# Attention and routed experts on one core: value products of a third query group in two parts, a pair of maxima and a transpose moved, and the last tiles taken two at a time

## The chip, the cores and the metric

The kernel runs on one core of a Trainium2 chip. The metric is device time in microseconds (us) of one execution; the kernel before takes 240.64 us, the median of 3 runs.

## What is computed

`x` is 2048 rows of 128 features. After a layer norm (`xn`), two branches are added to `x`: an attention over all 2048 rows with one head of 128 features, and a mixture of 8 experts of which each row takes two.

```python
xn = layernorm(x)
q, k, v = split(xn @ w_qkv.T)              # 2048 x 128 each
probs = softmax(q @ k.T / sqrt(8))
attn = swapaxes(probs @ v).reshape(...) @ w_proj.T + b_proj
t = xn @ W_in + b_in
gate: softmax(t @ W_gate + b_gate), the best two, normalised
moe = sum over the two experts of gate * (relu(t @ W1[e] + b1[e]) @ W2[e] + b2[e])
out = x + attn + (moe @ W_out + b_out)
```

## The kernel before

TensorE (PE) holds the order of the work, and the other engines have lists of their own that meet it at semaphores.

**Attention.** The 2048 queries are in six groups g: four of 256 (0 to 3) and two of 512 (4 and 5). A group is worked off in steps k (`STEPS`: 8 for a group of 256, 16 for one of 512), numbered i over the whole kernel, so group 2 is steps 16 to 23 and group 3 is steps 24 to 31. A step has 512 columns of scores: two blocks of 128 keys for a group of 256, one for a group of 512. In it PE does

- `scores(i)`: three products of a block of keys with the queries (lines 845 to 847). Numbers are kept as a high and a low part in fp32r: high times high, high times low, low times high.
- sometimes a *pair*, `pair(g + 1, m)` (line 906): raw scores of the next group, 128 queries by 1024 keys in two banks of PSUM. VectorE (DVE) takes the maximum of them (`pair_max`, line 618), and the next pair may only be written when that has been read (`max_read`), since all pairs of a later group use the same two banks. `PAIR_STEP[g]` lists in which steps the pairs stand; of two in one step the second stands behind the value products.
- `values(i - 2)`: the probabilities of two steps ago times the normed rows. In groups 0 to 3 this is one fp32 product for each block (line 970) of the probabilities `pf` that ScalarE (ACT) wrote (line 465). In groups 4 and 5 ACT writes the exponential twice, rounded to fp32r (`ph`, line 464) and whole (`pf`), DVE takes the difference `pl` (`low`, line 628), and PE does three fp32r products (lines 979, 980, 983).
- behind the last steps' work, the group before is finished: ACT copies its sums (`copy_u`, line 477), PE multiplies by the value weights (`out_rows`, line 997), DVE divides (`scale_out`, lines 634 and 637), PE multiplies by `w_proj` (`project`, line 1011), DVE adds (`add_out`, line 645).

**Routing.** GpSimd (POOL) sends the rows of `t` to slots in memory, sorted by expert, with 32 scatters (line 365), among them the additions of the bias (line 338) and the first four copies of expert weights (`stage`, line 355). When all scatters have landed, SyncE's queue (SP) loads the first tiles of slots (`load_xg`, line 266).

**Experts.** After group 3, 39 tiles of 128 slots go through the experts: a transpose of the tile (`xg_transpose`, line 1075, into one bank, so that each waits for ACT's copy of the one before; the first also waits until all maxima of group 4 are read), `layer1` (line 1087), `layer2` (line 1101). SP stores each result. Between group 3's last value products and the experts stand

```python
            values(BASE_B - 2)
            xg_transpose(0)
            xg_transpose(1)
            values(BASE_B - 1)
            layer1(0)
```

**The last part.** Groups 4 and 5 run on PE, and meanwhile POOL fetches the two results of each row back: for each of 16 tiles j two gathers (line 392) and the product of the one before with its first gate (`weigh`, line 387). DVE adds the second (`combine`, line 784). After the last `combine`, PE transposes the last four tiles (line 1134), DVE copies them (`cT`, line 815), and the last four row tiles are finished one by one (`last_scale`, lines 821 and 822; `last_add`, line 828; PE lines 1175, 1183, 1186). SP stores them in two transfers (line 289).

Of the kernel before, what the change touches and what calls it, by code (L numbers as in the profile page):

```python
# [7 lines left out]
ALU = mybir.AluOpType  # L8
# [4 lines left out]
def attention_moe_kernel(nc, x, w_qkv, w_proj, b_proj, w_in, b_in, w_gate, b_gate,  # L13
# [4 lines left out]
    P = 128  # L18
    S, D = x.shape[1], x.shape[2]
    NT = S // P  # L20
# [19 lines left out]
    PRE = 4  # L40
    WHOLE = 4

    PAIR_STEP = [[2, 4, 5, 6]] + 2 * [[1, 2, 4, 5]] + [[1, 2, 3, 4, 5, 6, 7, 7], [1, 3, 5, 6, 8, 9, 11, 12], []]
    NG = len(GROUPS)
# [10 lines left out]
    LAST = FIRST[NG]  # L55
    PLAIN = FIRST[WHOLE]

# [8 lines left out]
    def group_of(i):  # L66
        return max(g for g in range(NG) if FIRST[g] <= i)

    def pairs_at(g, k):
        return [m for m, at in enumerate(PAIR_STEP[g]) if at == k]  # L70

# [4 lines left out]

    BLOCK_AT = {14: 0, 21: 1, 28: 2}

    ctx = ExitStack()
    with ctx:  # L80
# [136 lines left out]

        def row_bank(c):  # L220
            return (MA, 0, 1, 2)[c]

        def sum_bank(c):
            return (MB, MX + 1, MA, 0)[c]

# [6 lines left out]
        def _(sp):  # L232
# [53 lines left out]
            for c in (2, 4):  # L286
                sp.wait_ge(Z["last_added"], c)
                a = NT - TB + c - 2
                sp.dma_start(ov[:, a:a + 2, :], x_sb[:, a:a + 2, :]).then_inc(Z["stored"], 16)
# [3 lines left out]
        def _(pool):  # L293
# [96 lines left out]
            for j in range(NT):  # L390
                for c in range(TOPK):
                    pool.indirect_dma_start(out=z[:, j, c, :], out_offset=None, in_=slots_out,  # L392
                                            in_offset=bass.IndirectOffsetOnAxis(ap=slots[:, c, j:j + 1], axis=0)
                                            ).then_inc(s_z[j], 16)
                if j >= 1:
                    weigh(j - 1)
            weigh(NT - 1)

        @block.scalar
        def _(act):  # L400
# [59 lines left out]
            def step(i):  # L460

                act.wait_ge(Z["st_done"], i + 1)
                if i >= PLAIN:
                    act.activation(ph[:, i % 3, :], ps[:, st_bank(i), :], ACT.Exp).then_inc(Z["ph_done"], 1)  # L464
                act.activation(pf[:, i % 3, :], ps[:, st_bank(i), :], ACT.Exp).then_inc(Z["pf_done"], 1)  # L465

            def copy_u(g):
                n = SIZE[g]
                act.wait_ge(Z["pv_done"], g + 1)
                if g >= 1:  # L470
                    act.wait_ge(Z["out_done"], FIRST_ROUND[g])
                parts = TILES[g] if g == NG - 1 else 1
                to = ut[:, 0:n].rearrange("e (p j) -> e j p", j=NT)
                of = ps[:, UB, 0:n].rearrange("e (j p) -> e j p", j=NT)
                for c in range(parts):
                    w = n // NT // parts
                    act.activation(to[:, :, w * c:w * (c + 1)], of[:, :, w * c:w * (c + 1)], ACT.Copy).then_inc(Z["ut_copied"], 1)
# [67 lines left out]
        def _(dve):  # L545
# [185 lines left out]
            for g in range(PRE):  # L731
                for k in range(STEPS[g]):
# [7 lines left out]
                    if k == PAIR_STEP[g][-1]:  # L740
                        row_max(g + 1)
                    if FIRST[g] + k >= PLAIN:
                        low(FIRST[g] + k)
# [36 lines left out]
            def combine(j):  # L780

                dve.wait_ge(s_z[j], 32)
                dve.wait_ge(Z["z_weighed"], j + 1)
                dve.scalar_tensor_tensor(out=z[:, j, 0, :], in0=z[:, j, 1, :], scalar=gate2[:, j:j + 1],
                                         in1=z[:, j, 0, :], op0=ALU.mult, op1=ALU.add).then_inc(Z["c_ready"], 1)
# [31 lines left out]

            def last_scale(c):
                n = FIRST_ROUND[NG - 1]
                dve.wait_ge(Z["out_done"], n + 1 + c)  # L820
                link("rinv", dve.reciprocal(rinv[:, c // 2, c % 2:c % 2 + 1], ps[:, row_bank(c), D:D + 1]))
                dve.tensor_scalar(o_sb[:, c // 2, c % 2, :], ps[:, row_bank(c), 0:D], rinv[:, c // 2, c % 2:c % 2 + 1], None,
                                  ALU.mult).then_inc(Z["o_ready"], 1)

            def last_add(c):
                at = x_sb[:, NT - TB + c, :]
                dve.wait_ge(Z["proj_done"], FIRST_ROUND[NG - 1] + c + 1)
                dve.tensor_tensor(at, ps[:, sum_bank(c), 0:D], at, ALU.add).then_inc(Z["last_added"], 1)

# [3 lines left out]
            last_scale(1)  # L833
            last_scale(2)
            last_add(0)
            last_scale(3)
            last_add(1)
            last_add(2)
            last_add(3)

        @block.tensor
        def _(pe):
# [116 lines left out]
            def values(i):  # L959
# [5 lines left out]
                elif first and g > 0:  # L965
                    pe.wait_ge(Z["ut_copied"], g)
                if g < WHOLE:
                    pe.wait_ge(Z["pf_done"], i + 1)
                    for h, c in enumerate(keys(i)):
                        last = pe.matmul(dst, xn[:, c, :], pf[:, i % 3, cols(g, h)], start=(first and h == 0),  # L970
                                         stop=(final and h == CH[g] - 1))
                    if final:
                        last.then_inc(Z["pv_done"], 1)
                    return
                pe.wait_ge(Z["ph_done"], i - PLAIN + 1)
                if g == WHOLE:
                    pe.wait_ge(Z["xnn_lo_ready"], keys(i)[-1] // TB + 1)
                for h, c in enumerate(keys(i)):
                    pe.matmul(dst, xn_hi[:, c, :], ph[:, i % 3, cols(g, h)], start=(first and h == 0), stop=False)
                    pe.matmul(dst, xn_lo[:, c, :], ph[:, i % 3, cols(g, h)], start=False, stop=False)  # L980
                pe.wait_ge(Z["lo_done"], i - PLAIN + 1)
                for h, c in enumerate(keys(i)):
# [189 lines left out]
            pe.wait_ge(Z["x_added"], NG - 1)  # L1172
            for c in range(TB):
                pe.wait_ge(Z["ut_copied"], NG + c)
                pe.matmul(ps[:, row_bank(c), 0:D + 2], ut[:, P * c:P * (c + 1)], wvT[:, :], start=True, stop=True
                          ).then_inc(Z["out_done"], 1)
# [7 lines left out]
            for c in range(TB):  # L1184
# [30 lines left out]
```

## Time and profile before

| | |
|---|---|
| median of 3 runs | 240.64 us (240.54 to 240.68) |
| the profiled execution, its own time | 240.99 us |
| its span, first to last instruction | 239.2 us |
| PE busy | 224.5 us, 94% |
| VectorE, ScalarE, GpSimd busy | 58%, 46%, 59% |
| granted clock of TensorE | full speed (its upper level, 2.4 GHz) in every slice |

Busy time of PE is the sum of its matmul records, whose ends are modelled, so a stretch that is full of work shows nearly 100%; what a stretch is worth is read from the starts of its rows. A record gives the duration of one matmul from its first column to its last result, while the next starts in its shadow: the distance between two starts is what a matmul costs. An fp32 matmul is two records. DMAs that SP and POOL issue have rows of their own; a gather or a scatter row is the time in which POOL makes its descriptors.

### The profile page before, as it was taken

How to read it: one execution, taken by the hardware profiler on the slowest of the kernel's cores; microseconds unless marked ns; L12 is line 12 of the kernel's file. 1: busy time of each engine (PE TensorE's matmuls, PEld its weight loads, DVE VectorE, ACT ScalarE, POOL GpSimd, SP SyncE). 2: the span in 40 equal slices, each digit the busy share in tenths (PEclk: the TensorE clock that was granted, in tenths of full speed). 3: DMA queues.
4: the chain of work that ended last, by engine and by line, in shares of the span. 5: the costliest groups of instructions: out<-in, count | busy, mean ns of one | idle time of the engine just before them, and what ended most of it. 6: DMA issues, size and time to landing. Idle time of an engine off the chain costs nothing.

```text
span 239.2 us, 4415 instructions
## 1 busy us (share of the span) xinstructions
PE 224.5 (94%) x1526; PEld 203.0 (85%) x1526; DVE 138.1 (58%) x332; ACT 110.1 (46%) x260; POOL 140.5 (59%) x163
## 2 busy tenths in 40 slices
PE   8798988999999997999999999999999989899974
PEld 8587876999999995899999999999977768688853
DVE  4988795552551754434445444445498885656644
ACT  2481432424325331544544444554466657667640
POOL 3249005888888850136666555666048888888830
PEclk9999999999999999999999999999999999999999
DMA  6799910111111103012222222222102111313121
GB/s 181 283 319 342 323 42 25 50 39 47 34 44 47 44 33 88 11 36 66 70 73 73 67 79 67 68 67 67 36 25 56 33 44 48 76 34 80 40 66 47
DMA packets 23046, 19.53 MB, mean 82 GB/s; under 512 B 3280, under 2 KB 19696, under 8 KB 22768
## 3 DMA queue, kind: packets, MB, share of 16 engines
q1 hardware_dynamic: 20000, 14.71, 20.3%
q0 software_dynamic: 2048, 4.20, 6.6%
q10 hardware_dynamic: 976, 0.33, 0.5%
q8 instruction: 13, 0.21, 0.3%
q14 instruction: 9, 0.07, 0.1%
HBM read 10.97 MB, written 8.26 MB: 80 GB/s over the span
## 4 chain that ended last, share of the span: by engine, by line
PE 59%; POOL 19%; DVE 9%; issue 6%; DMA 3%; ACT 2%; ACTq 1%; POOLq 0%; DVEq 0%
PE ps L1101 15%; PE ps L1087 15%; POOL wtab L392 14%; PE ps L970 9%; POOL wtab L387 5%; PE ps L906 4%; DVE part_max L618 4%; PE ps L845 3%; PE ps L847 3%; PE ps L846 3%; DMA w_raw<-in_L_attn_w_proj_dram 2%; PE ps L1075 2%; PE ps L872 1%; PE ps L997 1%; DMA slots_out<-y_sb 1%
## 5 line engine op out<-in xcount | busy, mean ns | idle before, releaser
L355 POOL COPY wst<-wtab 128x1156 f32 x39 | 44.9, 1151 | 39.7 <-DVE y_sb L766 39.7
L465 ACT ACTIVATE pf<-ps 128x512 f32<-128x512 f32 x64 | 38.1, 595 | 36.1 <-PE ps L847 32.5
L618 DVE TENSOR_REDUCE part_max<-ps 128x1 f32<-128x1024 f32 x32 | 38.8, 1222 | 13.2 <-PE ps L906 11.4
L365 POOL DMA_INDIRECT slots_in<-hl,slots x32 | 31.5, 985 | 20.1 <-DVE slots L698 13.2
L392 POOL DMA_INDIRECT wtab<-slots_out,slots x32 | 33.3, 1040 | 15.9 <-DMA slots_out<-y_sb 8.4
L1101 PE MATMUL ps<-wst,mid 128*128 128x128 f32 x312 | 41.3, 275 | 0.7 <-DVE x_sb L645 0.7
L1087 PE MATMUL ps<-xgT,wst 128*128 128x128 f32 x312 | 41.3, 275 | 0.0
L758 DVE TENSOR_SCALAR mid<-ps,wst 128x128 f32<-128x128 f32 x78 | 23.7, 346 | 29.7 <-PE ps L1087 29.7
L1101 PEld LDWEIGHTS ps<-wst,mid 128*128 128x128 f32 x312 | 38.0, 192 | 0.9 <-ACT mid L509 0.8
L1087 PEld LDWEIGHTS ps<-xgT,wst 128*128 128x128 f32 x312 | 38.0, 192 | 0.1
L845 PE MATMUL ps<-q_hi,xnT_hi 128*128 128x256 f32 (+1 forms) x96 | 35.6, 371 | 0.5 <-ACT q_hi L451 0.5
L970 PE MATMUL ps<-pf,xn 128*128 128x256 f32 x128 | 32.9, 379 | 0.0
L847 PE MATMUL ps<-q_lo,xnT_hi 128*128 128x256 f32 (+1 forms) x96 | 30.6, 318 | 0.0
L628 DVE TENSOR_TENSOR pl<-pf,ph 128x512 fp32r<-128x512 f32 x32 | 22.8, 713 | 13.3 <-ACT pf L465 11.9
L846 PE MATMUL ps<-q_hi,xnT_lo 128*128 128x256 f32 (+1 forms) x96 | 30.5, 317 | 0.0
L464 ACT ACTIVATE ph<-ps 128x512 fp32r<-128x512 f32 x32 | 19.2, 599 | 19.6 <-PE ps L847 18.1
L509 ACT ACTIVATE mid<-ps,wst 128x128 f32<-128x128 f32 x78 | 24.3, 363 | 7.5 <-PE ps L1087 7.5
L502 ACT ACTIVATE xgT<-ps 128x128 f32<-128x128 f32 x39 | 10.8, 278 | 34.7 <-PE ps L1075 34.7
L970 PEld LDWEIGHTS ps<-pf,xn 128*128 128x128 f32 x128 | 23.5, 189 | 3.6
L906 PE MATMUL ps<-xnT_hi,q_hi 128*128 128x512 f32 x64 | 21.0, 412 | 2.9 <-DVE part_max L618 2.4
L845 PEld LDWEIGHTS ps<-q_hi,xnT_hi 128*128 128x128 f32 x96 | 18.2, 189 | 2.3 <-ACT q_hi L451 0.7
L846 PEld LDWEIGHTS ps<-q_hi,xnT_lo 128*128 128x128 f32 x96 | 18.2, 189 | 1.6
(156 smaller groups left out, 309.5 us busy)
## 6 DMA issues: line engine op xcount, KB each, us to landing
wtab<-in_L_ffn_W_dram SPq DMA_DIRECT2D x16, 256.0 KB, 5.9
xg<-slots_in SPq DMA_DIRECT2D x39, 64.0 KB, 1.9
slots_out<-y_sb SPq DMA_DIRECT2D x39, 64.0 KB, 1.5
slots_in<-wst SPq DMA_DIRECT2D x2, 1024.0 KB, 4.9
x_sb<-in_L_attn_x_dram SPq DMA_DIRECT2D x4, 256.0 KB, 5.1
out_dram<-x_sb SPq DMA_DIRECT2D x3, 256.0 KB
wtab<-in_L_ffn_b_dram SPq DMA_DIRECT2D x1, 512.0 KB, 7.4
slots_in<-hl,slots POOLq DMA_INDIRECT x32
```

What stands on the lines that cost most here:

```text
L355: pool.tensor_copy(wst[:, t % 4, :], wtab[:, bass.ds(experts[t], 1), :].rearrange("p a n -> p (a n)")).then_inc(Z["staged"], 1)
L365: pool.indirect_dma_start(out=slots_in, out_offset=bass.IndirectOffsetOnAxis(ap=slots[:, c, j:j + 1], axis=0), in_=hl[:, j, 0:D], in_offse ...
L392: pool.indirect_dma_start(out=z[:, j, c, :], out_offset=None, in_=slots_out, in_offset=bass.IndirectOffsetOnAxis(ap=slots[:, c, j:j + 1], ...
L465: act.activation(pf[:, i % 3, :], ps[:, st_bank(i), :], ACT.Exp).then_inc(Z["pf_done"], 1)
L618: dve.tensor_reduce(part_max[:, g % 2, m // 2, m % 2:m % 2 + 1], ps[:, b:b + 2, :], AX.XY, ALU.max).then_inc(Z["max_read"], 1)
L845: pe.matmul(dst, lh, rh, start=start, stop=False)
L846: pe.matmul(dst, ll, rh, start=False, stop=False)
L847: return pe.matmul(dst, lh, rl, start=False, stop=stop)
L906: last = pe.matmul(ps[:, pair_bank(g, m) + b, :], q_hi[:, g % 2, P * t:P * (t + 1)], xnT_hi[:, at:at + BK], start=True, stop=True)
L970: last = pe.matmul(dst, xn[:, c, :], pf[:, i % 3, cols(g, h)], start=(first and h == 0), stop=(final and h == CH[g] - 1))
L1087: last = pe.matmul(ps[:, 2 * (t % 2) + h, SL * (c % 2):SL * (c % 2 + 1)], wst[:, t % 4, P * c:P * (c + 1)], xgT[:, t % 2, :], start=True, ...
L1101: last = pe.matmul(ps[:, y_bank(t), 0:D], mid[:, t % 2, c, :], wst[:, t % 4, DM + D * c:DM + D * (c + 1)], start=(c == 0), stop=(c == HC - 1))
```

## The change

Four edits are made together.

1. `WHOLE` becomes a set, groups 0, 1 and 3. Group 2 now splits its probabilities as groups 4 and 5 do; `splits(i)` counts the steps that do so.
2. In group 3, the list of pairs has its double step at step 6 where it was at step 7, and `values(BASE_B - 1)` stands between the first two transposes of slot tiles.
3. POOL weighs tiles 0 to 13; for tiles 14 and 15 DVE does it in `combine`.
4. The last four row tiles are scaled, projected and added two at a time, in one bank for two; the product with `wo_sb` stands beside the one with `wpT` that adds to it.

```diff
-    WHOLE = 4
+    WHOLE = (0, 1, 3)
-    PAIR_STEP = [[2, 4, 5, 6]] + 2 * [[1, 2, 4, 5]] + [[1, 2, 3, 4, 5, 6, 7, 7], [1, 3, 5, 6, 8, 9, 11, 12], []]
+    PAIR_STEP = [[2, 4, 5, 6]] + 2 * [[1, 2, 4, 5]] + [[1, 2, 3, 4, 5, 6, 6, 7], [1, 3, 5, 6, 8, 9, 11, 12], []]
+    def splits(i):
+        return sum(group_of(s) not in WHOLE for s in range(i + 1))
+    WEIGHED = 14
...
-                if j >= 1:
+                if 1 <= j <= WEIGHED:
                     weigh(j - 1)
-            weigh(NT - 1)
...
-                if i >= PLAIN:
+                if group_of(i) not in WHOLE:
                     act.activation(ph[:, i % 3, :], ps[:, st_bank(i), :], ACT.Exp).then_inc(Z["ph_done"], 1)
...
-                parts = TILES[g] if g == NG - 1 else 1
+                parts = ROUNDS[g] if g == NG - 1 else 1
...
-                    if FIRST[g] + k >= PLAIN:
+                    if g not in WHOLE:
                         low(FIRST[g] + k)
...
-                dve.wait_ge(Z["z_weighed"], j + 1)
+                if j < WEIGHED:
+                    dve.wait_ge(Z["z_weighed"], j + 1)
+                else:
+                    link("rinv", dve.tensor_scalar(z[:, j, 0, :], z[:, j, 0, :], gate1[:, j:j + 1], None, ALU.mult))
...
-            def last_scale(c):
+            def last_scale(r):
+                n = FIRST_ROUND[NG - 1] + r
+                rows = ps[:, row_bank(r), 0:2 * (D + 2)].rearrange("q (k d) -> q k d", d=D + 2)
+                dve.wait_ge(Z["out_done"], n + 1)
+                link("rinv", dve.reciprocal(rinv[:, n % 2, :], rows[:, :, D]))
+                dve.tensor_tensor(o_sb[:, n % 2, :, :], rows[:, :, 0:D], rinv[:, n % 2, :].unsqueeze(2).to_broadcast([P, 2, D]),
                                   ALU.mult).then_inc(Z["o_ready"], 1)
...
             last_scale(0)
             last_scale(1)
-            last_scale(2)
             last_add(0)
-            last_scale(3)
             last_add(1)
-            last_add(2)
-            last_add(3)
...
-                pe.wait_ge(Z["ph_done"], i - PLAIN + 1)
-                if g == WHOLE:
+                pe.wait_ge(Z["ph_done"], splits(i))
+                if g == min(set(range(NG)) - set(WHOLE)):
                     pe.wait_ge(Z["xnn_lo_ready"], keys(i)[-1] // TB + 1)
...
             xg_transpose(0)
+            values(BASE_B - 1)
             xg_transpose(1)
-            values(BASE_B - 1)
...
-            for c in range(TB):
-
-                if c >= 2:
-                    pe.wait_ge(Z["o_ready"], n + c - 1)
-                pe.matmul(ps[:, sum_bank(c), 0:D], cT[:, P * c:P * (c + 1)], wo_sb[:, :], start=True, stop=False)
-            for c in range(TB):
-                pe.wait_ge(Z["o_ready"], n + 1 + c)
-                pe.matmul(ps[:, sum_bank(c), 0:D], o_sb[:, c // 2, c % 2, :], wpT[:, :], start=False, stop=True
-                          ).then_inc(Z["proj_done"], 1)
+            for r in range(ROUNDS[NG - 1]):
+
+                pe.wait_ge(Z["o_ready"], n + r + 1)
+                for k in range(2):
+                    at = P * (2 * r + k)
+                    pe.matmul(ps[:, sum_bank(r), P * k:P * (k + 1)], cT[:, at:at + P], wo_sb[:, :], start=True, stop=False)
+                    last = pe.matmul(ps[:, sum_bank(r), P * k:P * (k + 1)], o_sb[:, (n + r) % 2, k, :], wpT[:, :], start=False, stop=True)
+                last.then_inc(Z["proj_done"], 1)
```

TensorE's list at the end of group 3, before: from the pair of step 7 (line 906) to the first `layer1` (line 1087). Line 970 is a value product, line 1075 a transpose of slots.

```order
L906 MATMUL ps<-xnT_hi,q_hi 128x512 x2
L970 MATMUL ps<-pf,xn 128x256 x2
L906 MATMUL ps<-xnT_hi,q_hi 128x512 x2
L970 MATMUL ps<-pf,xn 128x256 x2
L1075 MATMUL ps<-ident,xg 128x128 x2
L970 MATMUL ps<-pf,xn 128x256 x2
L1087 MATMUL ps<-xgT,wst 128x128 x4
```

The same place now, from the second pair of step 6; lines 850 to 852 are the scores of step 31, line 911 a pair, 975 value products, 1080 a transpose, 1092 `layer1`.

```order
L911 MATMUL ps<-xnT_hi,q_hi 128x512 x2
L850 MATMUL ps<-q_hi,xnT_hi 128x256
L851 MATMUL ps<-q_hi,xnT_lo 128x256
L852 MATMUL ps<-q_lo,xnT_hi 128x256
L850 MATMUL ps<-q_hi,xnT_hi 128x256
L851 MATMUL ps<-q_hi,xnT_lo 128x256
L852 MATMUL ps<-q_lo,xnT_hi 128x256
L911 MATMUL ps<-xnT_hi,q_hi 128x512 x2
L975 MATMUL ps<-pf,xn 128x256 x4
L1080 MATMUL ps<-ident,xg 128x128
L975 MATMUL ps<-pf,xn 128x256 x2
L1080 MATMUL ps<-ident,xg 128x128
```

Behind the last pair stood one step's value products; two steps' stand there now, and the last step's are between the transposes.

VectorE's list in steps 1 to 4 of group 2, now. Line 622 is a maximum of a pair, 632 the new `low`, 638 and 641 the division (`scale_out`), 649 `add_out`; before, the same list stood there without the rows of `pl`.

```order
L622 TENSOR_REDUCE part_max<-ps 128x1
L632 TENSOR_TENSOR pl<-pf,ph 128x512
L622 TENSOR_REDUCE part_max<-ps 128x1
L632 TENSOR_TENSOR pl<-pf,ph 128x512
L638 RECIPROCAL rinv<-ps 128x2
L641 TENSOR_TENSOR o_sb<-ps,rinv 128x256
L632 TENSOR_TENSOR pl<-pf,ph 128x512
L649 TENSOR_TENSOR x_sb<-ps,x_sb 128x256
L622 TENSOR_REDUCE part_max<-ps 128x1
```

So the division of group 1 stands behind the difference of step 2, and the addition behind that of step 3.

## Rows read from the trace of the kernel before

**Rows 1.** The page: span, then busy us and share of each engine
```profile
span 239.2 us, 4415 instructions
PE 224.5 (94%) x1526; PEld 203.0 (85%) x1526; DVE 138.1 (58%) x332; ACT 110.1 (46%) x260; POOL 140.5 (59%) x163
```

**Rows 2.** The chain that ended last: start us, us, what
```profile
173.44 1.52 DMA slots_out<-y_sb
...
175.92 0.99 POOL wtab L392
...
228.99 1.84 issue
```

**Rows 3.** Timeline, PE, group 2, steps 1 to 3: start us, us, line
```profile
61.13 1.03 PE L970 MATMUL ps<-pf,xn 128*128 128x256 f32 x4
61.81 0.47 PE L845 MATMUL ps<-q_hi,xnT_hi 128*128 128x256 f32 x1
62.12 0.28 PE L846 MATMUL ps<-q_hi,xnT_lo 128*128 128x256 f32 x1
...
62.71 0.64 PE L906 MATMUL ps<-xnT_hi,q_hi 128*128 128x512 f32 x2
63.18 1.02 PE L970 MATMUL ps<-pf,xn 128*128 128x256 f32 x4
...
66.07 0.61 PE L1011 MATMUL ps<-wpT,o_sb 128*128 128x128 f32 x4
```

**Rows 4.** Timeline, DVE, the same steps
```profile
63.38 1.23 DVE L618 TENSOR_REDUCE part_max<-ps 128x1 f32<-128x1024 f32 x1 [0.82 <-PE ps L906]
...
64.90 0.42 DVE L637 TENSOR_TENSOR o_sb<-ps,rinv 128x256 f32<-128x256 f32 x1
```

**Rows 5.** Lines 628, 387 and 392, all their instructions: ns min/median/max
```profile
L628 DVE TENSOR_TENSOR pl<-pf,ph x32: 676/692/930, 173.4 to 229.1; 128x512 fp32r<-128x512 f32 x32
...
L387 POOL TENSOR_SCALAR wtab<-wtab,gate x16: 602/760/1082, 181.2 to 230.9; 128x128 f32<-128x128 f32 x16
...
L392 POOL DMA_INDIRECT wtab<-slots_out,slots x32: 944/1001/1462, 175.9 to 227.2; - x32
```

**Rows 6.** Timeline, PE, end of group 3
```profile
88.11 0.64 PE L906 MATMUL ps<-xnT_hi,q_hi 128*128 128x512 f32 x2
...
92.11 0.73 PE L906 MATMUL ps<-xnT_hi,q_hi 128*128 128x512 f32 x2 [0.45 <-DVE part_max L618]
92.68 1.02 PE L970 MATMUL ps<-pf,xn 128*128 128x256 f32 x4
94.25 0.30 PE L1075 MATMUL ps<-ident,xg 128*128 128x128 f32 x1 [0.55 <-DVE part_max L618]
95.01 0.30 PE L1075 MATMUL ps<-ident,xg 128*128 128x128 f32 x1 [0.46 <-ACT xgT L502]
95.15 1.03 PE L970 MATMUL ps<-pf,xn 128*128 128x256 f32 x4
96.01 1.05 PE L1087 MATMUL ps<-xgT,wst 128*128 128x128 f32 x8
```

**Rows 7.** Timeline, SP, first eight slot loads; page, DMA issues, last number us to landing
```profile
88.85 3.66 SPq L266 DMA_DIRECT2D xg<-slots_in  x8
...
xg<-slots_in SPq DMA_DIRECT2D x39, 64.0 KB, 1.9
```

**Rows 8.** Timeline, all engines, the tail
```profile
230.89 0.60 POOL L387 TENSOR_SCALAR wtab<-wtab,gate 128x128 f32<-128x128 f32 x1 [1.89 <-DMA wtab<-slots_out,slots]
231.59 0.35 DVE L784 SCALAR_TENSOR_TENSOR wtab<-wtab,gate 128x128 f32<-128x128 f32 x1 [1.50 <-POOL wtab L387]
...
232.69 0.69 DVE L815 COPY cT<-ps 128x512 f32<-128x512 f32 x1 [0.75 <-PE ps L1134]
...
235.92 0.49 PE L1186 MATMUL ps<-wpT,o_sb 128*128 128x128 f32 x2 [0.40 <-DVE o_sb L822]
...
236.45 0.29 DVE L828 TENSOR_TENSOR x_sb<-ps,x_sb 128x128 f32<-128x128 f32 x1 [0.19 <-PE ps L1186]
```

More of the change, by code:

```diff
@@ L55, in attention_moe_kernel @@
     LAST = FIRST[NG]
-    PLAIN = FIRST[WHOLE]
     BY_DVE = [2, 2, 3, 3]
@@ L216, in hl_banks, with row_bank, sum_bank @@
             return ps[:, b:b + 2, 0:2 * HW].rearrange("p b (j n) -> p b j n", n=HW)
[L220 to L224, printed above, removed]
+        def row_bank(r):
+            return (MA, 0)[r]
+        def sum_bank(r):
+            return (MB, MX + 1)[r]
         def y_bank(t):
@@ L285, in _ @@
                 sp.dma_start(ov[:, a:b, :], x_sb[:, a:b, :]).then_inc(Z["stored"], 16)
-            for c in (2, 4):
-                sp.wait_ge(Z["last_added"], c)
-                a = NT - TB + c - 2
+            for r in range(ROUNDS[NG - 1]):
+                sp.wait_ge(Z["last_added"], r + 1)
+                a = NT - TB + 2 * r
                 sp.dma_start(ov[:, a:a + 2, :], x_sb[:, a:a + 2, :]).then_inc(Z["stored"], 16)
@@ L815, in _, with last_add @@
             dve.tensor_copy(cT[:, :], ps[:, MX, :]).then_inc(Z["cT_copied"], 1)
-            def last_scale(c):
[L819 to L822, printed above, removed]
-                                  ALU.mult).then_inc(Z["o_ready"], 1)
[L825 to L828, printed above, removed]
+            def last_scale(r):
[4 more added lines that the diff above has]
+                dve.tensor_tensor(o_sb[:, n % 2, :, :], rows[:, :, 0:D], rinv[:, n % 2, :].unsqueeze(2).to_broadcast([P, 2, D]),
+                                  ALU.mult).then_inc(Z["o_ready"], 1)
+            def last_add(r):
+                at = x_sb[:, NT - TB + 2 * r:NT - TB + 2 * r + 2, :]
+                dve.wait_ge(Z["proj_done"], FIRST_ROUND[NG - 1] + r + 1)
+                dve.tensor_tensor(at, ps[:, sum_bank(r), 0:2 * D].rearrange("p (j e) -> p j e", e=D), at, ALU.add
+                                  ).then_inc(Z["last_added"], 1)
             dve.wait_ge(Z["proj_done"], FIRST_ROUND[NG - 1])
@@ L966, in values @@
                     pe.wait_ge(Z["ut_copied"], g)
-                if g < WHOLE:
+                if g in WHOLE:
                     pe.wait_ge(Z["pf_done"], i + 1)
@@ L980, in values @@
                     pe.matmul(dst, xn_lo[:, c, :], ph[:, i % 3, cols(g, h)], start=False, stop=False)
-                pe.wait_ge(Z["lo_done"], i - PLAIN + 1)
+                pe.wait_ge(Z["lo_done"], splits(i))
                 for h, c in enumerate(keys(i)):
@@ L1172, in _ @@
             pe.wait_ge(Z["x_added"], NG - 1)
-            for c in range(TB):
-                pe.wait_ge(Z["ut_copied"], NG + c)
-                pe.matmul(ps[:, row_bank(c), 0:D + 2], ut[:, P * c:P * (c + 1)], wvT[:, :], start=True, stop=True
-                          ).then_inc(Z["out_done"], 1)
+            for r in range(ROUNDS[NG - 1]):
+                pe.wait_ge(Z["ut_copied"], NG + r)
+                for k in range(2):
+                    at = P * (2 * r + k)
+                    last = pe.matmul(ps[:, row_bank(r), (D + 2) * k:(D + 2) * (k + 1)], ut[:, at:at + P], wvT[:, :], start=True, stop=True)
+                last.then_inc(Z["out_done"], 1)
             pe.wait_ge(Z["cT_copied"], NR)
             pe.wait_ge(Z["moe_added"], NR - 1)
-            for c in range(TB):
-                if c >= 2:
-                    pe.wait_ge(Z["o_ready"], n + c - 1)
-                pe.matmul(ps[:, sum_bank(c), 0:D], cT[:, P * c:P * (c + 1)], wo_sb[:, :], start=True, stop=False)
-            for c in range(TB):
-                pe.wait_ge(Z["o_ready"], n + 1 + c)
-                pe.matmul(ps[:, sum_bank(c), 0:D], o_sb[:, c // 2, c % 2, :], wpT[:, :], start=False, stop=True
-                          ).then_inc(Z["proj_done"], 1)
+            for r in range(ROUNDS[NG - 1]):
+                pe.wait_ge(Z["o_ready"], n + r + 1)
+                for k in range(2):
+                    at = P * (2 * r + k)
+                    pe.matmul(ps[:, sum_bank(r), P * k:P * (k + 1)], cT[:, at:at + P], wo_sb[:, :], start=True, stop=False)
+                    last = pe.matmul(ps[:, sum_bank(r), P * k:P * (k + 1)], o_sb[:, (n + r) % 2, k, :], wpT[:, :], start=False, stop=True)
+                last.then_inc(Z["proj_done"], 1)
 _INS = ['L0_attn_x', 'L0_attn_w_qkv', 'L0_attn_w_proj', 'L0_attn_b_proj', 'L0_ffn_W_in', 'L0_ffn_b_in',
```

## The prediction

> **What bounds the kernel now.** I read the page first: PE is busy 94% of a span of 239.2 us [rows 1]. A share over the whole says too little, so next the chain of waits, in order of time. It has three parts. Up to 173 us it is PE almost throughout: groups 0 to 3, then the 39 expert tiles. At 173.44 the last result goes to memory, and from 175.92 to 228.99 the chain is POOL's 32 gathers with 15 products between them [rows 2]; the steps of groups 4 and 5 run beside them and end a little earlier. Then comes the tail, from the landing of the last gather to the last addition [rows 8]. So an edit counts if it shortens PE's list before 173 us (all that follows is released by the last expert tile and moves with it) or the tail. For both I read the timeline engine by engine. The profiled execution took 240.99 us, 1.79 more than its span and 0.35 more than the median of 240.64; I take differences from its rows and subtract them from the median.
>
> **Group 2 in parts.** Before, a step's values are two fp32 products, 4 records. From the start at 61.13 to the scores at 61.81 are 0.68 us, and the first score product holds on 0.31 us (to 62.12) where the next five take (62.71 - 62.12) / 5 = 0.118: together 0.68 + 0.19 = 0.87 us [rows 3]. After, they are 6 fp32r products of 256 columns, the form of the scores: 6 x 0.118 = 0.71. That saves 0.16 a step, 8 x 0.16 = 1.28 us.
>
> What it adds lies on other engines. ACT: 8 more exponentials, of 0.6 us, which it has room for (busy 46% [rows 1]); the pair of step 1 needs the next queries' high part from behind one of them, and has some 0.2 us to spare by my count. DVE: 8 times `low`, median 0.69 [rows 5], in order between the pairs' maxima. Three places are close:
>
> - Step 2: the maximum starts at 63.38 [rows 4]. The `low` of step 1 stands ahead of it, behind a maximum that began one step of 2.05 us earlier and ended at 61.33 + 1.23 = 62.56, and so ends near 63.3: no delay.
> - Step 3: `project` started at 66.07 [rows 3]; two steps of shorter values would bring it to 65.75. It needs the division, which now stands behind the `low` of step 2. Before, the product of the division was over at 64.90 + 0.42 = 65.32 [rows 4]; a `low` in line costs some 0.55 to 0.62 (the next operation starts before its end), so 65.87 to 65.94. PE waits 0.15 to 0.2.
> - The next pair in the following step can start 0.67 (from pair to maximum, 62.71 to 63.38) + 1.23 + 0.06 (a hop) = 1.96 us after the one before [rows 3, 4]. The step was 2.05 long and becomes 1.89: 0.07 of waiting, in step 5 of group 2 and step 2 of group 3.
>
> The `low` of a step is done over a step before `values` asks for it. Together 1.28 - 0.15 - 0.14 = 1.0 us. Bounds: 1.3 if nothing waits; 0.2 if each `low` delays a maximum by its slack and more.
>
> **Pairs and transposes at the end of group 3.** Before, the last pair starts at 92.11, values of step 30 at 92.68 and end 0.86 later (two fp32 products) at 93.54; PE is then idle to 94.25, since the first transpose waits for the last maximum, and the second transpose waits for ACT until 95.01; then values (95.15) and `layer1` (96.01) [rows 6]. After: the pair of step 5 stays at 88.11 in this count. The second pair of step 6 waits for its maximum until 88.11 + 1.96 = 90.07 and takes 0.57 as a pair that was waited for (92.11 to 92.68 [rows 6]; 0.47 otherwise, 62.71 to 63.18 [rows 3]), scores 0.71 to 91.35; its maximum runs 90.84 to 92.06, so the last pair starts at 92.12, as before. Behind it now stand two values of 0.86 (92.69 to 94.41), which cover the maximum (over at 94.1), the transpose 0.14, values to 95.41, which cover ACT's copy, the transpose 0.14: `layer1(0)` at 95.55, 0.46 sooner. The second `layer1` waited for ACT, whose copy of the transposed tile stands behind `copy_u`; now 0.2 us more of it is covered. I count 0.6. The waiting has not gone: the new double step waits twice, 0.6 and 0.8 us, for the maxima; what is won is that nothing waits behind the last one. Bounds 0.3 and 0.9.
>
> What this may run into: the transpose now comes at 94.4 - 1.0 = 93.4. The slots' loads are issued from 88.85 on [rows 7], when the scatters have landed, which PE does not hasten; they land 1.9 us later [rows 7], 90.8. Slack 2.6 us.
>
> **Tiles 14 and 15 weighed by DVE.** The last data are seen at 230.89; POOL's product takes 0.60, DVE starts at 231.59 and is over at 231.94 [rows 8]. On DVE, a product by a scalar is between 0.29 and 0.35 (its additions and products of 128 columns), and then a hop of 0.04: start of its second half at 231.28, end at 231.63. It saves 0.3 us; bounds 0 and 0.4. Tile 14's product lies before that, in time that DVE has.
>
> **Two tiles at a time.** Let T be the end of the copy of `cT`, 232.69 + 0.69 = 233.38; the last addition ends at 236.45 + 0.29 = 236.74, T + 3.36 [rows 8]. After: reciprocal from T - 0.08, division of 256 columns 0.42 (as in [rows 4]) over at T + 0.55; PE at T + 0.61. It then does four fp32 products of 128 columns, 0.22 each: 0.88. From the start of one to the addition are 236.45 - 235.92 = 0.53 [rows 8], so for four 0.53 + 3 x 0.22 = 1.19. The second four start at T + 1.49, their addition at T + 2.68, 0.42 long: T + 3.1. It saves 0.26 us. The products with `wo_sb`, which before ran while DVE divided, now wait for it; this is inside the sum. Bounds: -0.3 and 0.6.
>
> **Sum.** 1.0 + 0.6 + 0.3 + 0.25 = 2.15 us, 240.64 - 2.15 = 238.5 us.
>
> **A rule weighed.** Rows: DVE's `low` takes 0.68 to 0.93, POOL's product 0.60 to 1.08, its gathers 0.94 to 1.46 [rows 5]: where both work, one is sometimes held for up to half a microsecond. In group 2 there is now `low` beside POOL's bias additions and copies, before only beside gathers. The Trainium skill, page "SBUF — State Buffer", section "SBUF: two separate sides", says that a DVE operation with two inputs in SBUF and a GpSimd operation that reads SBUF exclude each other for their whole length. The trace agrees as far as its spreads go. By the rule, each of the eight `low` could hold POOL, or be held, for a whole operation.
>
> **Rivals.**
>
> *DVE eats the gain of group 2 (chance 0.15).* If `low` meets POOL's operations, it takes 0.93 in place of 0.69 [rows 5], and the maximum behind it is late by the surplus; four of them and a longer wait in step 3 cost 0.24 x 4 = 1.0 of the 1.28. Against it: DVE's median is at its minimum. Time: 240.64 - 1.2 = 239.4.
>
> *More is won (0.15).* No waits in group 2 (1.3), `layer1` 0.9 sooner, tail 0.8: 237.6.
>
> *The scatters become late (0.07).* POOL is held, by 1.08 - 0.60 = 0.48 for each of eight `low`, 3.8 us; slack 2.6 + 1.0 of gain given back: `layer1` starts with the gain of group 2 and of the transposes lost. Time: 240.64 - 0.55 = 240.1. Against it: most bias additions are over before step 4 of group 2.
>
> *The gathers get longer (0.06, the other side).* The chain from 175.92 to 228.2 is 32 gathers whose single lengths go from 0.94 to 1.46 [rows 5]. If their rhythm against DVE's changes, each gather that falls from 1.00 to 1.46 costs 0.46; from five more on (2.15 / 0.46) the kernel is not faster, with eight it takes 242. Against it: both sides start from the same event as before, and the new DVE operations of this part come behind the last gather.
>
> *As summed, 0.57.* Its own range is 238.0 to 239.0.
>
> **How the numbers follow.** The point is the likeliest case, 238.5. The range reaches to the richer and the poorer case, 237.5 to 239.5; outside are half of the cases at its ends and most of the last two. A measurement here tells 0.2%, 0.48 us, from nothing. Faster by more: 0.57 + 0.15 + 0.15 and some of the late scatters, 0.90; slower 0.04; the same 0.06.
>
> **What would show it.** The start of the first `layer1` (96.01 [rows 6]) at 94.5 with the first transpose behind no wait for a maximum; the start of `project` in step 3 of group 2 near 65.9 and a wait before it; the last result's way to memory ([rows 2], 173.44) at 171.8; the gathers' stretch as long as before, 53 us; from the last landing to the last addition 5.3 us where it was 5.85. I am wrong if a new wait for DVE stands at the pairs of group 2, if the loads of slots release the first transpose, or if the gathers' stretch is over 54.

## The result and the profile after

The changed kernel takes 238.91 us, the median of 4 runs (238.74 to 238.95), beside 240.6 us for the kernel before. The ratio is 0.9927, with a 95% interval of 0.9916 to 0.9939: 1.7 us faster. Forecast were 2.15 us and a range of 237.5 to 239.5. Some executions show a lower granted clock: at 0.99 they took 1.1 to 1.4 us more than the median of their kernel, and one of e9, at 0.855, took 257.19 us and is left out; the executions called undisturbed below are those with 0.997 or more.

The page of the changed kernel: span, busy time, clock.

```profile
span 236.8 us, 4445 instructions
...
PE 223.8 (95%) x1542; PEld 203.6 (86%) x1542; DVE 143.3 (61%) x336; ACT 113.9 (48%) x266; POOL 140.7 (59%) x161
...
PEclk9999999999999999999999999999999999999999
```

The span fell by 2.4 us, the time of that same execution from 240.99 to 238.74, by 2.25, and the median only by 1.7. Two things lie between. The profiled execution before took 0.4 us more than its median; in it TensorE began the scores 0.22 us later than in this one, which has to be taken off each comparison of start times below. And the time that lies outside the span (time of an execution less its span) was larger: 2.07 us in the median of the four executions (1.94 in the profiled one), where the kernel before has 1.79. The experiments come back to this.

TensorE in group 2, timeline of the changed kernel; line 984, 985 and 988 are the new value products, 1016 is `project`.

```profile
60.42 0.62 PE L911 MATMUL ps<-xnT_hi,q_hi 128*128 128x512 f32 x2
...
62.93 0.28 PE L984 MATMUL ps<-ph,xn_hi 128*128 128x256 f32 x1
...
63.64 0.61 PE L1002 MATMUL ps<-wvT,ut 128*128 128x130 f32 x4
...
65.29 0.40 PE L988 MATMUL ps<-pl,xn_hi 128*128 128x256 f32 x2
65.56 0.71 PE L1016 MATMUL ps<-wpT,o_sb 128*128 128x128 f32 x4
...
68.59 0.28 PE L852 MATMUL ps<-q_lo,xnT_hi 128*128 128x256 f32 x1
68.77 0.73 PE L911 MATMUL ps<-xnT_hi,q_hi 128*128 128x512 f32 x2
69.33 0.28 PE L984 MATMUL ps<-ph,xn_hi 128*128 128x256 f32 x1
...
76.00 0.63 PE L911 MATMUL ps<-xnT_hi,q_hi 128*128 128x512 f32 x2
...
77.95 0.74 PE L911 MATMUL ps<-xnT_hi,q_hi 128*128 128x512 f32 x2
78.53 1.03 PE L975 MATMUL ps<-pf,xn 128*128 128x256 f32 x4
```

The same places in the kernel before:

```profile
60.66 0.63 PE L906 MATMUL ps<-xnT_hi,q_hi 128*128 128x512 f32 x2
...
69.75 1.02 PE L970 MATMUL ps<-pf,xn 128*128 128x256 f32 x4
...
76.98 0.63 PE L906 MATMUL ps<-xnT_hi,q_hi 128*128 128x512 f32 x2
...
79.50 1.03 PE L970 MATMUL ps<-pf,xn 128*128 128x256 f32 x4
```

From the first pair beside group 2 to the value products behind the second pair beside group 3, a stretch with all eight steps of group 2's values in it, are 78.53 - 60.42 = 18.11 us; before they were 79.50 - 60.66 = 18.84. Group 2 gained 0.73 us.

A step's values are 63.64 - 62.93 = 0.71 us, as reckoned. What a step saves is a little less than reckoned. Where TensorE waits for nothing, four steps in a row last 76.00 - 69.33 = 6.67 us and lasted 76.98 - 69.75 = 7.23: 0.14 a step, not 0.16. The three waits are to be seen by rows that got longer: `project` in step 3 lasts 0.71 where an unhindered one lasts 0.61 (as in [rows 3]), and the pairs at 68.77 and 77.95 last 0.73 and 0.74 where others last 0.63. What follows such a pair starts 0.56 to 0.58 us behind it, not 0.47: after a wait TensorE loses about 0.1 us more, beyond the wait. The waits themselves are short. A product of 256 columns holds TensorE 0.12 us here, so it is free at 65.29 + 0.24 = 65.53 and at 68.59 + 0.12 = 68.71: 0.03 us of waiting at `project` and 0.06 at the pair, and 0.06 at the other pair too.

VectorE in the same steps.

```profile
62.23 0.82 DVE L632 TENSOR_TENSOR pl<-pf,ph 128x512 fp32r<-128x512 f32 x1
63.13 1.22 DVE L622 TENSOR_REDUCE part_max<-ps 128x1 f32<-128x1024 f32 x1
64.27 0.70 DVE L632 TENSOR_TENSOR pl<-pf,ph 128x512 fp32r<-128x512 f32 x1
64.89 0.16 DVE L638 RECIPROCAL rinv<-ps 128x2 f32<-128x2 f32 x1
65.08 0.42 DVE L641 TENSOR_TENSOR o_sb<-ps,rinv 128x256 f32<-128x256 f32 x1
```

It has become one unbroken row of work in step 2: the division is over at 65.50, and TensorE, which could have gone on at 65.53, starts at 65.56.

GpSimd beside it, all instructions of its scatters and of VectorE's difference, ns minimum, median, maximum; then single rows of both and the loads of slots in the timeline.

```profile
L370 POOL DMA_INDIRECT slots_in<-hl,slots x32: 962/986/1257, 37.3 to 87.7; - x32
```
```profile
L632 DVE TENSOR_TENSOR pl<-pf,ph x40: 674/693/1137, 59.8 to 227.5; 128x512 fp32r<-128x512 f32 x40
```
```profile
60.18 0.66 POOL L343 TENSOR_TENSOR x_sb<-x_sb,bsum 128x128 f32<-128x128 f32 x1
...
62.65 1.25 POOL L370 DMA_INDIRECT slots_in<-hl,slots  x1 [0.17 <-issue]
...
68.06 0.96 POOL L370 DMA_INDIRECT slots_in<-hl,slots  x1 [0.30 <-issue]
...
68.63 0.68 DVE L632 TENSOR_TENSOR pl<-pf,ph 128x512 fp32r<-128x512 f32 x1
...
89.93 3.66 SPq L271 DMA_DIRECT2D xg<-slots_in  x8
```

A scatter that begins while VectorE's difference runs takes 1.23 to 1.26 us where others take 0.96 to 0.99; there are four of them (at 62.65, 64.57, 66.49 and 71.62). One bias addition took 0.66 where others take 0.46 to 0.48. These five make 1.3 us. A scatter that was already running when the difference began held nothing: the one at 68.06 took 0.96 and the difference at 68.63 took 0.68. The loads of slots start at 89.93 instead of 88.85 [rows 7], 1.1 us later by the rows and 1.3 with the earlier start of this execution. They still land (89.93 + 1.9 = 91.8) before TensorE wants the first, at 93.42: of the slack of 2.6 us, 1.6 are left.

TensorE at the end of group 3.

```profile
89.09 0.72 PE L911 MATMUL ps<-xnT_hi,q_hi 128*128 128x512 f32 x2 [0.45 <-issue]
...
91.13 0.73 PE L911 MATMUL ps<-xnT_hi,q_hi 128*128 128x512 f32 x2 [0.61 <-DVE part_max L622]
91.70 1.89 PE L975 MATMUL ps<-pf,xn 128*128 128x256 f32 x8
93.42 0.27 PE L1080 MATMUL ps<-ident,xg 128*128 128x128 f32 x1
93.53 1.03 PE L975 MATMUL ps<-pf,xn 128*128 128x256 f32 x4
94.40 0.27 PE L1080 MATMUL ps<-ident,xg 128*128 128x128 f32 x1
94.51 1.06 PE L1092 MATMUL ps<-xgT,wst 128*128 128x128 f32 x8
```

From the pair of step 5 (87.14; before 88.11 [rows 6]) to the first `layer1` are 7.37 us; before they were 7.90. The waits behind the last pair are gone, the two before it are there.

The chain of the changed kernel from the last expert tile on, and its end.

```profile
171.82 1.52 DMA slots_out<-y_sb
...
174.30 0.99 POOL wtab L397
...
225.61 3.44 DMA wtab<-slots_out,slots
229.07 0.30 DVE wtab L790
229.39 0.36 DVE wtab L791
...
233.92 0.42 DVE x_sb L836
```

The last tile's store is 1.62 us earlier than in [rows 2], 1.4 without the earlier start, and the gathers take as long as before (174.30 to 226.56, 52.3 us). In the tail, VectorE takes the landed data at 229.07 and has them weighed and added at 229.74, 0.67 us, where GpSimd and VectorE took 1.05 [rows 8]. From the end of the copy of `cT` (230.49 + 0.69) to the last addition's end are 3.16 us, before 3.36.

Of the signs named in the prediction, `project` in step 3 came at 65.56, 65.78 without the earlier start, for 65.9. The first `layer1` (94.51 for 94.5), the last tile's store (171.82 for 171.8), the gathers' stretch (52.3 for 53) and the way from the last landing to the last addition (229.07 to 234.34, 5.27 for 5.3) came out. The closeness of the first two is luck: without the earlier start of 0.22 us they stand at 94.73 and 172.04, which goes with the smaller gain.

### The profile page after: what moved, and what is told of

Same layout as the page of the kernel before. It is cut to its first block, busy times and chain, and to the rows that moved or that the text cites. A ratio compares the mean times of both kernels' runs of the same rounds, so it can differ in the third digit from the quotient of the medians.

```text
span 236.8 us, 4445 instructions
## 1 busy us (share of the span) xinstructions
PE 223.8 (95%) x1542; PEld 203.6 (86%) x1542; DVE 143.3 (61%) x336; ACT 113.9 (48%) x266; POOL 140.7 (59%) x161
## 4 chain that ended last, share of the span: by engine, by line
PE 61%; POOL 18%; DVE 9%; issue 5%; DMA 4%; ACTq 1%; POOLq 1%; ACT 1%; DVEq 0%
PE ps L1106 15%; PE ps L1092 15%; POOL wtab L397 13%; PE ps L975 7%; POOL wtab L392 5%; PE ps L911 5%; DVE part_max L622 4%; PE ps L850 3%; PE ps L852 3%; PE ps L851 3%; DMA w_raw<-in_L_attn_w_proj_dram 2%; PE ps L1080 2%; PE ps L858 2%; DMA wtab<-slots_out,slots 1%; PE ps L877 1%
## 5 line engine op out<-in xcount | busy, mean ns | idle before, releaser
L370 POOL DMA_INDIRECT slots_in<-hl,slots x32 | 32.6, 1018 | 20.1 <-DVE slots L702 13.1
L632 DVE TENSOR_TENSOR pl<-pf,ph 128x512 fp32r<-128x512 f32 x40 | 28.9, 723 | 19.9 <-ACT pf L469 18.6
L468 ACT ACTIVATE ph<-ps 128x512 fp32r<-128x512 f32 x40 | 24.0, 600 | 25.5 <-PE ps L852 22.2
L850 PE MATMUL ps<-q_hi,xnT_hi 128*128 128x256 f32 (+1 forms) x96 | 34.5, 359 | 0.5 <-ACT q_hi L455 0.5
L975 PE MATMUL ps<-pf,xn 128*128 128x256 f32 x96 | 24.4, 379 | 0.0
L975 PEld LDWEIGHTS ps<-pf,xn 128*128 128x128 f32 x96 | 17.6, 189 | 2.7
L770 DVE TENSOR_TENSOR y_sb<-ps,wst 128x128 f32<-128x128 f32 x39 | 11.4, 292 | 13.4 <-PE ps L1106 13.4
```

Source lines behind the costliest of these rows:

```text
L370: pool.indirect_dma_start(out=slots_in, out_offset=bass.IndirectOffsetOnAxis(ap=slots[:, c, j:j + 1], axis=0), in_=hl[:, j, 0:D], in_offse ...
L850: pe.matmul(dst, lh, rh, start=start, stop=False)
```

## Experiments

Times are medians beside the kernel before on the same chip, another chip for each set of four. It had 240.76 us there for the first four (e1 to e4), 240.55 for the next four (e5 to e8) and 240.56 for the last four (e9 to e12). "Faster" by some us is the difference of the two medians; the ratio is the measured one with its 95% interval.

**e1: only the split of group 2.**

```diff
-    WHOLE = 4
+    WHOLE = (0, 1, 3)
```
(with `splits(i)` and the conditions that follow from it)

> The kernel before with the probabilities of group 2 in two parts, nothing else. Theory (from the two traces: 8 x 0.16 us saved, three new waits for VectorE at 0.07 to 0.15 us, each with 0.1 us more in which TensorE starts anew): 0.7 us faster than before, 239.9. My prediction's working had 1.0 us (239.6). Rival (VectorE eats all of it): 0.3 or less.

Measured: 240.03 us, 0.73 faster; ratio 0.996 (0.994 to 0.998). The interval, 0.5 to 1.4 us, does not part 0.7 from the forecast 1.0; the rows do. The stretch that was 18.84 us before and is 18.11 in the changed kernel is 18.10 here (60.63 to 78.73), 0.74 less.

**e2: only the end of group 3, both edits.**

```diff
-[1, 2, 3, 4, 5, 6, 7, 7]
+[1, 2, 3, 4, 5, 6, 6, 7]
...
-            xg_transpose(1)
             values(BASE_B - 1)
+            xg_transpose(1)
```

> The kernel before with the double step of pairs at step 6 and the value products between the transposes, nothing else. Theory: 0.6 us faster (the last maximum and the copy of the first tile lie under value products), 240.0. Rival: 0, if the loads of the slots or the copy of the group's sums end the wait in any case.

Measured: 240.11 us, 0.65 faster; 0.9969 (0.9956 to 0.9982).

**e9: of these, only the place of the value products.**

```diff
-            xg_transpose(1)
             values(BASE_B - 1)
+            xg_transpose(1)
```

> The kernel before with the value products of step 31 between the two transposes, and the pairs as they were. Theory: this alone does it. The first transpose comes at 94.25 as before (it waits for the last maximum), then 0.14 + 0.86 + 0.14 give the first layer1 at 95.4, where both edits together gave 95.5: 0.65 to 0.75 us faster than before, and moving the pair cost about 0.1. Rival (my prediction's reading, that the pair's move covers the last maximum and gives part of the gain): 0.4 us or less.

Measured: 239.75 us in the median of five executions, 0.81 faster; 0.9966 (0.9953 to 0.9979). TensorE in this kernel:

```profile
87.87 0.64 PE L906 MATMUL ps<-xnT_hi,q_hi 128*128 128x512 f32 x2
...
91.89 0.73 PE L906 MATMUL ps<-xnT_hi,q_hi 128*128 128x512 f32 x2 [0.45 <-DVE part_max L618]
92.46 1.02 PE L970 MATMUL ps<-pf,xn 128*128 128x256 f32 x4
94.03 0.30 PE L1075 MATMUL ps<-ident,xg 128*128 128x128 f32 x1 [0.55 <-DVE part_max L618]
94.16 1.03 PE L970 MATMUL ps<-pf,xn 128*128 128x256 f32 x4
95.03 0.27 PE L1075 MATMUL ps<-ident,xg 128*128 128x128 f32 x1
95.14 1.06 PE L1087 MATMUL ps<-xgT,wst 128*128 128x128 f32 x8
```

The first transpose still waits 0.55 us for the last maximum, as in [rows 6], and yet `layer1` comes 95.14 - 87.87 = 7.27 us behind the pair of step 5, 0.1 sooner than the 7.37 with both edits (e2 has 7.36). The times of e9 and e2 differ the same way, by 0.16, with intervals that overlap. The whole gain is the 0.76 us between the two transposes (94.25 to 95.01 in [rows 6]), under which value products now lie. The pair's move gives nothing: with it, TensorE waits once more before a pair and once less before a transpose.

**e3: only the weighing by VectorE.**

```diff
-            weigh(NT - 1)
...
+                    link("rinv", dve.tensor_scalar(z[:, j, 0, :], z[:, j, 0, :], gate1[:, j:j + 1], None, ALU.mult))
```

> The kernel before with the last two tiles weighed by VectorE, nothing else. Theory: the product takes 0.28 us on VectorE in place of 0.60 on GpSimd, with the hop 0.38 faster, 240.2. My prediction had 0.3. Rival: up to 0.55, if VectorE also sees the landing of the gather earlier than GpSimd did (0.18 in the trace).

Measured: 240.27 us, 0.49 faster; 0.9974 (0.9962 to 0.9986). VectorE in its tail:

```profile
230.60 0.28 DVE L786 TENSOR_SCALAR wtab<-wtab,gate 128x128 f32<-128x128 f32 x1 [0.19 <-DMA wtab<-slots_out,slots]
230.93 0.35 DVE L787 SCALAR_TENSOR_TENSOR wtab<-wtab,gate 128x128 f32<-128x128 f32 x1
```

From the landing to the end of `combine` 0.68 us, before 1.05: 0.37. The rest, 0.1, is within the interval. From the last gather's end to the start of the product the traces have 2.42 to 2.69 us with GpSimd and 2.41 to 2.61 with VectorE, which is no ground to say that VectorE sees the landing sooner.

**e4: only the last four row tiles two at a time.** The edits of `last_scale`, `last_add`, `copy_u` and of the last products, as in the diff of the change.

> The kernel before with the last four row tiles scaled, projected and added two at a time, nothing else. Theory: 0.2 us faster (3.16 in place of 3.36 us behind the copy of cT), 240.4. Rival: nothing or slower, since the products with wo_sb wait for the division.

Measured: 241.0 us; ratio 1.0012 (0.9995 to 1.003): no gain, and 0.2 us of loss in the medians, where 0.2 of gain was expected. Yet in its rows the stretch from the end of the copy of `cT` to the end of the last addition is 3.16 us long, as in the changed kernel. The rows and the time disagree, and most of the difference lies outside the span (table below).

**e10: the last divisions in pairs, the additions one by one.**

```diff
-                pe.wait_ge(Z["o_ready"], n + 1 + c)
-                pe.matmul(ps[:, sum_bank(c), 0:D], o_sb[:, c // 2, c % 2, :], wpT[:, :], start=False, stop=True
+                pe.wait_ge(Z["o_ready"], n + 1 + c // 2)
+                pe.matmul(ps[:, sum_bank(c), 0:D], o_sb[:, (n + c // 2) % 2, c % 2, :], wpT[:, :], start=False, stop=True
```
(with the paired `last_scale` of the change; the four products with `wo_sb` stay ahead in four banks)

> The kernel before with the copy, the products and the division of the last four row tiles two at a time, but with the additions one at a time as before. Theory A (the time outside the span grows by 0.2 us with the wide additions): the part outside stays at 1.8 us, and the time falls with the span. Theory B (it is the wide copy and division, or anything that this tail changes): 1.95 or more outside the span.

Measured: 240.23 us, 0.33 faster; 0.9981 (0.9969 to 0.9992); outside the span 1.79 us, as before. VectorE in its tail:

```profile
232.41 0.69 DVE L815 COPY cT<-ps 128x512 f32<-128x512 f32 x1 [0.75 <-PE ps L1133]
...
234.98 0.96 DVE L829 TENSOR_TENSOR x_sb<-ps,x_sb 128x128 f32<-128x128 f32 x4 [0.80 <-PE ps L1187]
```

The stretch from the copy to the last addition is 235.94 - 233.10 = 2.84 us, 0.52 less than before and 0.32 less than with both in pairs. In this kernel the products with `wo_sb` still run while VectorE divides. The time has 0.33 of the 0.52: from the last addition to the end of the span are 2.56 us here, 2.46 before, and where the other 0.1 lies is not followed up.

**e11: the last additions in pairs, the divisions one by one.**

```diff
-            for c in range(TB):
-                pe.wait_ge(Z["o_ready"], n + 1 + c)
+            for r in range(ROUNDS[NG - 1]):
+                for k in range(2):
+                    c = 2 * r + k
+                    pe.wait_ge(Z["o_ready"], n + 1 + c)
```
(with the paired `last_add` of the change, `wo_sb` beside `wpT` in one bank)

> The kernel before with the last additions two tiles at a time from one bank, each product with wo_sb beside the one with wpT, but the divisions one at a time. Theory A: 1.95 us or more outside the span. Theory B: 1.8 us outside it. The span itself should be within 0.3 us of before, rather longer, since all products with wo_sb wait for a division.

Measured: 240.81 us, 0.25 slower; 1.0017 (1.0004 to 1.0031). Its span is 0.2 us shorter than that of before (238.6 beside 238.8), where it was expected rather longer, and its rows from the copy of `cT` to the last addition last 3.09 us; its time is longer. Time less span, over the undisturbed executions of each kernel (spans are on record to 0.1 us, so single values are good to 0.05):

```
kernel                       executions   median   least to most
before (beside e1 to e4)         27         1.79    1.71 to 1.86
before (beside e5 to e8)          9         1.75    1.72 to 1.90
before (beside e9 to e12)        21         1.77    1.71 to 1.86
e1, e2, e3                    8, 11, 12     1.81, 1.79, 1.78   1.71 to 1.88
e9                                5         1.75    1.73 to 1.79
e10, divisions paired            11         1.79    1.70 to 1.85
e11, additions paired             9         2.13    2.04 to 2.21
e4, both paired                  10         1.96    1.74 to 2.78
changed kernel                    4         2.07    1.94 to 2.11
e5                                5         1.92    1.78 to 2.32
e6                                5         1.99    1.83 to 2.35
e7                                4         1.88    1.82 to 2.07
e8                                4         2.02    1.92 to 2.14
e12                               4         1.83    1.73 to 1.89
```

Between e10 and e11, theory A of the two stands: the part outside grew with the form of the last products and additions, and not with the division. It is not the additions in pairs alone. e7 and e12 have them too, and 1.88 and 1.83 us; e4 has them, and its executions scatter from 1.74 to 2.78. The mechanism is open. In the timelines the rows of the two last stores, taken together, last 1.22 or 1.23 us in e4, e5, e6, e11 and the changed kernel, and 0.81 to 1.01 in the others: the second store is left further behind the first.

```profile
235.36 1.22 SPq L289 DMA_DIRECT2D out_dram<-x_sb  x2
235.80 0.42 DVE L828 TENSOR_TENSOR x_sb<-ps,x_sb 128x256 f32<-128x256 f32 x1 [0.47 <-PE ps L1184]
```

These are e11's. That this distance is the cause is no more than a guess: e8 and e12 have the same tail and 1.00 us there, and 2.02 and 1.83 outside. What lies outside the span, no row shows.

**e5: the division ahead of the difference in step 2 of group 2.**

```diff
-                    if g not in WHOLE:
+                    if g not in WHOLE and k != 2:
                         low(FIRST[g] + k)
...
+                    if g not in WHOLE and k == 2:
+                        low(FIRST[g] + k)
```

> The changed kernel with VectorE's division of group 1 ahead of the difference of step 2 of group 2. Theory (a project that waits for the division costs its wait and 0.1 us of a new start): 0.2 us faster than the changed kernel, 238.7, and the project row of step 3 back at 0.61 us. Rival (this wait is hidden): no difference.

Measured: 238.6 us; 0.9914 (0.99 to 0.9927) to the kernel before. The changed kernel was not timed beside it; the two ratios differ by 0.0013, 0.3 us, with intervals that overlap. The rows say 0.13 (0.2 was expected): `project` is back at 0.61 us,

```profile
65.60 0.61 PE L1018 MATMUL ps<-wpT,o_sb 128*128 128x128 f32 x4
```

and from the first pair beside group 2 to the first beside group 3 TensorE needs 15.45 us (60.49 to 75.94), the changed kernel 15.58 (60.42 to 76.00).

**e6: the pairs beside group 2 in steps 1, 2, 3 and 5.**

```diff
-    PAIR_STEP = [[2, 4, 5, 6]] + 2 * [[1, 2, 4, 5]] + ...
+    PAIR_STEP = [[2, 4, 5, 6], [1, 2, 4, 5], [1, 2, 3, 5]] + ...
```

> The changed kernel with the pairs beside group 2 in steps 1, 2, 3 and 5. Between two pairs there is then always more than the value products of one step, and project stands behind a pair. Theory: the wait of the pair of step 5 (0.07 + 0.1) and that of project (0.1 + 0.1) go: 0.3 to 0.4 us faster than the changed kernel, 238.55. Rival: no difference, or a new wait since the division now stands between two maxima.

Measured: 238.68 us; 0.9921 (0.9908 to 0.9935). The medians can't tell this from the changed kernel (0.9927). The same stretch is 15.27 us (60.51 to 75.78), 0.31 less than the 15.58: both waits are gone, and 0.31 is their 0.03 and 0.06 with the 0.1 of a new start behind each, to 0.02.

```profile
64.89 0.63 PE L911 MATMUL ps<-xnT_hi,q_hi 128*128 128x512 f32 x2
...
66.06 0.61 PE L1016 MATMUL ps<-wpT,o_sb 128*128 128x128 f32 x4
```

**e7: a product with `wo_sb` of each last round ahead of the wait.**

```diff
+                        if r == 0:
+                            pe.matmul(ps[:, sum_bank(1), 0:P], cT[:, 2 * P:3 * P], wo_sb[:, :], start=True, stop=False)
+                        pe.wait_ge(Z["o_ready"], n + r + 1)
```
(the first round's own, of its first tile, stands ahead of it too)

> The changed kernel with the first product with wo_sb of each of the two last rounds ahead of the wait for the division. Theory: two of eight fp32 products of 128 columns (0.22 us each) leave the stretch from the division to the last addition: 0.44 us faster than the changed kernel, 238.5. Rival: 0.2 or less, if the second division is what the second round waits for.

Measured: 238.19 us; 0.9903 (0.9887 to 0.9918), 0.0024 below the changed kernel's ratio, 0.6 us. In the rows, the copy of `cT` to the last addition is 2.65 us (231.21 to 233.86), 0.5 less than 3.16; the rest may be the time outside the span, 1.88 us beside 2.07.

**e8: e5, e6 and e7 together.**

> The changed kernel with the last three edits together. Theory: 0.35 + 0.44 = 0.8 us faster than the changed kernel, 238.1 (the division's place no longer matters where the pair stands ahead of project). Rival: less than 0.5, if one edit brings back the wait of another.

Measured: 238.02 us; 0.9895 (0.988 to 0.991), 0.0032 below the changed kernel's ratio, 0.8 us, as expected.

**e12: e8 with the pair's double step back at step 7.**

```diff
-[1, 2, 3, 4, 5, 6, 6, 7]
+[1, 2, 3, 4, 5, 6, 7, 7]
```

> The changed kernel with the three edits tried before (division ahead of the difference, pairs in steps 1, 2, 3, 5, the first products with wo_sb ahead of the wait) and the pair's double step put back to step 7. If moving the pair cost 0.1 us, this is 0.1 us faster than the same kernel without the last edit (238.02), 237.9; the first layer1 about 0.1 us sooner. Rival: 0.3 us slower than that, if the pair's move was worth something.

Measured: 237.7 us; 0.9886 (0.9871 to 0.9901), the fastest here, 2.9 us faster than before and 1.0 (by the ratios) than the changed kernel. Against e8 its ratio is 0.0009 lower, 0.2 us, with intervals that overlap, and part of that can be the time outside the span, 1.83 beside 2.02; by the rows, the first `layer1` comes 7.26 us behind the pair of step 5, in e8 7.39. That is the 0.1 us that e9 showed.

## Why the prediction was right, and where it was not

**The sum.** Alone, the four edits give 0.73 + 0.65 + 0.49 - 0.24 = 1.63 us, together 1.7. By their intervals each of the four is known to 0.3 to 0.5 us only, so the sum shows no sign that they disturb one another, and no more than that. Forecast were 1.0 + 0.6 + 0.3 + 0.25 = 2.15. The total came out inside the range with one term too small by 0.2 and two too large by 0.3 and 0.5. All is released by the last expert tile, as said: the gathers moved with it and kept their length.

**Group 2: 0.73 for 1.0.** That the steps get shorter, and the three places of waiting, were right. Three terms were mis-sized. The saving was reckoned as 0.16 a step, and the rows have 0.14 to 0.15: some 1.15 us in all for 1.28. The waits were reckoned as 0.15 to 0.2 and twice 0.07, and are 0.03 and twice 0.06: 0.15 for 0.29. And the new start behind each of the three was put at nothing, which cost 0.1 each: 0.3 us, the largest of the errors. I had its price before me, 0.57 us in place of 0.47 for a pair that was waited for [rows 6], and used it only for the pairs at the end of group 3. With these the sum is 1.15 - 0.15 - 0.30 = 0.7, which the rows of e1 have; e5 and e6 show the waits' part by taking them away. The prediction also named "a new wait for DVE stands at the pairs of group 2" as a sign of being wrong, although its own sum has one of 0.07 there; the wait stands there, at 68.77, and is no such sign.

**The end of group 3: 0.65 for 0.6.** The size was right, one reason was not. The step that failed is "Behind it now stand two values of 0.86, which cover the maximum": they do, but the two pairs moved together wait as long before the last pair as the transpose waited behind it. e9 has the gain without the move. I reckoned only the two edits together; the same rows gave, for the second alone, 94.25 + 0.14 + 0.86 + 0.14 = 95.39, sooner than the 95.55 of both.

**The weighing: 0.49 for 0.3.** The product is 0.28 us on VectorE, just under what I took (0.29 to 0.35), and this makes 0.37 in the rows. The rest, 0.1, the rows don't show; it is within the noise.

**Two at a time: nothing or a loss for 0.25.** The rows shortened by 0.20, nearly as reckoned. What failed was a premise that stood before the terms, "I take differences from its rows and subtract them from the median": it takes the 1.79 us outside the span to be the same for both kernels. e11 shows it grown by 0.35 us; e10 keeps it and has 0.33 us of gain. That the rows themselves gave no more than 0.20 has a cause that can be seen: the divisions in pairs alone have 0.52, and e7, which puts two products with `wo_sb` back ahead of the waits, has 0.5 more than the changed kernel. The edit won time at VectorE and gave most of it back by making those products wait.

**The rule weighed, and the rivals.** The Trainium skill, page "SBUF — State Buffer", section "SBUF: two separate sides", has a VectorE operation with two inputs in SBUF and a GpSimd operation that reads SBUF exclude each other for a whole operation, whichever began first. The rows agree in part. GpSimd's bias addition and the four scatters that began under a difference grew by 0.19 to 0.28 us, and the difference at 70.87, which began under a copy of GpSimd, took 1.14, 0.45 more than the median; each grew by 0.11 to 0.15 us less than the overlap of the two rows, as a wait for the rest of the other operation would give. But a scatter that was already running did not hold the difference: at 68.63 the overlap is 0.39 us and the difference took 0.68. There the measurement decides; whether a scatter reads SBUF over its whole length, or only at its start, no row shows. So the late scatters were real, 1.3 us of a feared 3.8, and the slack of 2.6 us hid them. The gathers did not get longer, and the waits for VectorE with the new starts ate 0.45 of the gain of group 2, not 1.0.

## What to carry to other kernels

When an edit moves two things, reckon each alone from the same rows: here one of two moves had all the gain and by the rows the other cost 0.1 us. Count a wait of an engine that runs without gaps at its length and the new start behind it, 0.1 us for TensorE here. When products are put together with others that wait, ask what they ran beside until then: here that gave back most of a gain of 0.5 us. At the very end of a kernel, a span that shrinks is not yet a time that shrinks: compare time less span over several executions before believing rows of the tail.

## What the runs showed of the hardware

The time outside the span, 1.70 to 1.90 us in 104 executions of kernels with single last additions (57 of them of the kernel before), was 2.04 to 2.21 us in the 9 of the kernel with paired ones and nothing else (e11), though its last store is of the same size; in the other kernels with paired additions it was 1.73 to 2.78 us, so the pairing alone does not set it. An indirect scatter of GpSimd went from 0.98 to 1.25 us when it began under a VectorE subtraction with both inputs in SBUF, and such a subtraction that began under a running scatter kept its 0.68 us. After a wait of 0.03 to 0.06 us in a stream without gaps TensorE lost another 0.1 us: its next product came 0.56 to 0.58 us behind a pair instead of 0.47.
